# The neighbour sum with every 64th step fetched row by row from SyncE's queue

## The reference

```python
h = jnp.maximum(_layernorm(x, axis=-1), 0.0)
msgs = h[src]
neigh = jax.ops.segment_sum(msgs, dst, num_segments=h.shape[0])
h = (1.0 + eps[0]) * h + neigh
h = jax.nn.relu(h @ W1 + b1)
x = x + (h @ W2 + b2)
```

## Time and profile before

| | us |
|---|---|
| median of 3 runs (4853.4 to 4856.95) | 4854.46 |
| the profiled execution | 4847.91 |
| its span, first to last instruction | 4845.8 |
| GpSimd busy | 3416.4 (71% of the span) |
| DVE busy | 2778.0 (57%) |
| ACT busy | 2159.0 (45%) |
| PE busy | 476.5 (10%) |

### The profile page before, as it was taken

The page is one execution under the profiler, slowest core; times in us unless marked ns, Lnnn a source line. Parts: engine busy times, 40 slices in busy tenths (PEclk is TensorE's granted clock), DMA queues, the critical chain, the costliest instruction groups (busy, mean ns, idle before and its releaser), DMA issues.

```text
span 4845.8 us, 21987 instructions
## 1 busy us (share of the span) xinstructions
PE 476.5 (10%) x2321; PEld 339.9 (7%) x2321; DVE 2778.0 (57%) x4395; ACT 2159.0 (45%) x2238; POOL 3416.4 (71%) x3611
## 2 busy tenths in 40 slices
PE   4620000000000000000189000000000000000005
PEld 2410000000000000000067000000000000000003
DVE  7836888988998988888778222222222222222224
ACT  4414445544455555544367344444444444444431
POOL 4676777777777777777554677777777777777766
PEclk9655555555555555555599555555555555555558
DMA  9995666666666666666455233333333333333324
GB/s 360 382 372 171 211 210 217 212 212 213 213 213 213 214 215 213 214 213 213 139 118 124 94 104 103 103 105 104 103 102 102 102 102 107 103 102 103 104 98 136
DMA packets 235399, 816.50 MB, mean 168 GB/s; under 512 B 67021, under 2 KB 93677, under 8 KB 185162
## 3 DMA queue, kind: packets, MB, share of 16 engines
q1 hardware_dynamic: 77464, 457.58, 24.7%
q0 software_dynamic: 143152, 344.65, 24.3%
q10 hardware_dynamic: 14722, 13.70, 0.9%
HBM read 455.06 MB, written 354.21 MB: 167 GB/s over the span
## 4 chain that ended last, share of the span: by engine, by line
POOL 59%; issue 26%; DMA 8%; PE 5%; DVE 2%; ACT 1%; POOLq 0%; SPq 0%; ACTq 0%; DVEq 0%
POOL arena L632 58%; DMA q_edges<-arena 6%; PE ps L1285 2%; PE ps L1274 2%; DMA arena<-states,node_idx 1%; POOL q_edges L636 0%; PE ps L1306 0%; ACT arena L1119 0%; POOLq L120 0%; PE ps L1265 0%; PE ps L1298 0%; SPq L529 0%; DVE arena L1914 0%; DMA arena<-h_tab,idx 0%; DVE arena L1701 0%
## 5 line engine op out<-in xcount | busy, mean ns | idle before, releaser
L632 POOL DMA_INDIRECT arena<-h_tab,idx x1568 | 1482.0, 945 | 520.5 <-issue 500.2
L632 POOL DMA_INDIRECT arena<-kv_tab,idx x1568 | 1485.1, 947 | 514.5 <-issue 503.5
L1874 DVE SCALAR_TENSOR_TENSOR ps<-arena,keep,ps 128x128 f32<-128x128 f32 x98 | 42.9, 438 | 1500.8 <-ACT ps L1162 1500.8
L1162 ACT COPY ps<-arena 128x2048 f32<-128x2048 f32 x98 | 351.6, 3587 | 948.1 <-DMA arena<-h_tab,idx 948.1
L1066 ACT COPY arena<-arena 128x1024 f32<-128x1024 f32 x196 | 375.6, 1916 | 552.3 <-DVE arena L1701 552.3
L1586 DVE TENSOR_TENSOR_SCAN ps<-arena,ps 128x256 f32<-128x256 f32 (+2 forms) x584 | 501.4, 859 | 0.0
L1169 ACT COPY arena<-arena 128x1024 f32<-128x1024 f32 x196 | 379.1, 1934 | 212.9 <-DVE arena L1882 212.9
L1882 DVE TENSOR_TENSOR_SCAN arena<-arena,ps 128x1024 f32<-128x1024 f32 x196 | 437.5, 2273 | 10.4 <-DVE ps L1874 0.5
L1701 DVE TENSOR_TENSOR_SCAN arena<-arena,ps 128x1024 f32<-128x1024 f32 x196 | 442.9, 2260 | 0.1
L1033 ACT COPY ps<-arena 128x1024 f32<-128x1024 f32 x196 | 363.5, 1887 | 6.1
L1637 DVE TENSOR_TENSOR arena<-arena,ps 128x1024 f32<-128x1024 f32 x196 | 230.4, 1217 | 178.2 <-DMA arena<-kv_tab,idx 178.2
(11 more groups left out here) (240 smaller groups left out, 2380.2 us busy)
## 6 DMA issues: line engine op xcount, KB each, us to landing
states<-arena SPq DMA_DIRECT2D x98, 1152.0 KB, 5.4
q_edges<-arena SPq DMA_DIRECT2D x98, 1024.0 KB, 5.9
arena<-q_edges SPq DMA_DIRECT2D x98, 1024.0 KB, 7.8
states<-arena SPq DMA_DIRECT2D x98, 1024.0 KB, 4.0
arena<-kv_tab,idx POOLq DMA_INDIRECT x1568, 2.8
arena<-h_tab,idx POOLq DMA_INDIRECT x1568, 2.5
kv_tab<-arena ACTq DMA_DIRECT2D x14, 896.0 KB, 11.2
arena<-kv_tab SPq DMA_DIRECT2D x14, 448.0 KB, 5.4
```

Of the source, the lines that this page charges most:

```text
L632: pool.indirect_dma_start(to, None, tab, bass.IndirectOffsetOnAxis(ap=at, axis=0)).then_inc(done, 16)
L1162: nc.scalar.copy(rows_now, rows[k].rearrange("p b f -> p f b")).then_inc(rows_turned, 1)
```

## The change

In each of 24 batches (5, 9, 13, ..., 97: the second of every four, except batch 1) the last of the 16 steps is not gathered by GpSimd. Its 128 rows come through SP, each with a DMA of its own from `h2_tab` to one partition of a small buffer `direct`.

- SP writes the 24 x 128 row numbers once, at the start of stage B, to a table `direct_tab` in memory (L558 of the changed kernel).
- In stage D SP reads 16 of them at a time to registers (`direct_rows`) and issues 16 DMAs of one row. 32 rows stand between two stores. The rows of batch 4q + 5 are fetched while batches 4q to 4q + 2 are stored.
- ACT waits for `direct_in` in those batches, and turns the step and the other 15 with two copies.
- GpSimd's loop now goes over four batches, behind four that are written out.
- Some semaphores of stage C and E are shared (`node_rows_in`, `node_tiles_in`), with counts that go on.

```diff
+QUADS = BATCHES // 4
+DIRECT_AT = 4 * B + 2 * B - 1
+AT_ONCE = 16
+PARTS = P // AT_ONCE
...
+        direct_tab = dram("direct_tab", [QUADS, P], I32)
...
+        direct = cD.two(HID)
+        direct_listed, direct_in = sem("direct_listed"), sem2("direct_in")
...
             sp.dma_start(qb[0], q_rows[:, 0:B, :]).then_inc(q_in[0], 16)
+            sp.dma_start(direct_tab.rearrange("t p -> p t"), src_all[:, DIRECT_AT:STEPS:4 * B], allow_slow_non_contiguous=True)\
+                .then_inc(direct_listed, 16)
...
+            def store_d(n, k):
+                sp.wait_ge(sums_set, n + 1)
+                settle(sp)
+                sp.dma_start(by_step(states1)[:, bass.ds(n * B, B), :], sums_b[k]).then_inc(sums_out[k], 16)
+
+            def direct_rows(q, t, part):
+
+                p0 = part * AT_ONCE
+                src_rows = nc.values_load_multi_w_load_instructions(
+                    direct_tab[bass.ds(q, 1), p0:p0 + AT_ONCE], engines=[mybir.EngineType.SP], min_val=0, max_val=N - 1,
+                    skip_runtime_bounds_check_because="edges name nodes")[1]
+                for r, row in enumerate(src_rows):
+                    sp.dma_start(direct[t][p0 + r:p0 + r + 1, :], h2_tab[bass.ds(row, 1), :]).then_inc(direct_in[t], 16)
+
+            def quads_d(i, first):
+                for t in range(2):
+                    q = i * 2 + t
+                    if not first:
+                        sp.wait_ge(rows_turned, q * 4 - 2)
+                    for r in range(4):
+                        if not (first and t == 0 and r == 0):
+                            store_d(q * 4 + r - 1, (r + 1) % 2)
+                        for part in range(r * PARTS // 4, (r + 1) * PARTS // 4):
+                            direct_rows(q, t, part)
+            sp.wait_ge(direct_listed, 16)
+            for k in range(2):
+                sp.wait_ge(h2_stored[k], 16 * PAIRS)
+            repeat(sp, QUADS // 2, quads_d)
+            for n in range(4 * QUADS - 1, BATCHES):
+                store_d(n, n % 2)
...
-            repeat(pool, BPAIRS, batch_d)
+            for r in range(4):
+                batch_d(r, r % 2, B, r < 2)
+            with pool.Fori(1, QUADS) as i:
+                for r in range(4):
+                    batch_d(i * 4 + r, r % 2, B - (r == 1))
+            for r in range(2):
+                batch_d(4 * QUADS + r, r % 2, B - (r == 1))
...
+                act.wait_ge(rows_in[k], landed)
+                act.wait_ge(sum_s, n * 2 + 1)
+                if direct_t is None:
                     nc.scalar.copy(rows_now, rows[k].rearrange("p b f -> p f b")).then_inc(rows_turned, 1)
+                else:
+                    act.wait_ge(direct_in[direct_t], direct_landed)
+                    nc.scalar.copy(rows_now[:, :, B - 1], direct[direct_t])
+                    nc.scalar.copy(rows_now[:, :, 0:B - 1], rows[k][:, 0:B - 1, :].rearrange("p b f -> p f b"))\
+                        .then_inc(rows_turned, 1)
```

More of the change, by code:

```diff
@@ L57 @@
 EREST = E - EFULL * STEPS
+QUADS = BATCHES // 4
+DIRECT_AT = 4 * B + 2 * B - 1
+AT_ONCE = 16
+PARTS = P // AT_ONCE
+assert BATCHES == 4 * QUADS + 2 and QUADS % 2 == 0
 BPAIRS = BATCHES // 2
@@ L921, in _, with batch_d @@
                 pool.wait_ge(h2_stored[k], 16 * PAIRS)
[L923 to L931, removed]
-            repeat(pool, BPAIRS, batch_d)
+            def batch_d(n, k, steps, peeled=False):
+                pool.wait_ge(idx1_set, n + 1)
+                if not peeled:
+                    pool.wait_ge(rows_turned, n - 1)
+                settle(pool)
+                for b in range(steps):
+                    gather(rows[k][:, b, :], h2_tab, idx[k][:, b:b + 1], rows_in[k])
+            for r in range(4):
[5 more added lines that the diff above has]
+                batch_d(4 * QUADS + r, r % 2, B - (r == 1))
             for k in range(2):
@@ L1155, in _ @@
             keep1_features(0, 0)
[L1157 to L1161, removed]
-                    nc.scalar.copy(rows_now, rows[k].rearrange("p b f -> p f b")).then_inc(rows_turned, 1)
[L1163 to L1171, removed]
@@ L1172, in _, with batch_d @@
-            repeat(act, BPAIRS, batch_d)
+            DIRECT_WAIT = 16 * P
+            def batch_d(n, k, landed, direct_t=None, direct_landed=None, stored=None):
+                act.wait_ge(rows_in[k], landed)
+                act.wait_ge(sum_s, n * 2 + 1)
+                if direct_t is None:
+                    nc.scalar.copy(rows_now, rows[k].rearrange("p b f -> p f b")).then_inc(rows_turned, 1)
+                else:
[3 more added lines that the diff above has]
+                        .then_inc(rows_turned, 1)
+                nc.scalar.copy(idx[k][:], src_all[:, bass.ds((n + 2) * B, B)]).then_inc(idx1_set, 1)
+                keep1_features(n + 1, 1 - k)
+                if stored is not None:
+                    act.wait_ge(sums_out[k], stored)
+                for half in range(2):
+                    act.wait_ge(sum_s, n * 2 + half + 2)
+                    done = nc.scalar.copy(sums_b[k][:, :, half * HF:(half + 1) * HF].rearrange("p b f -> p f b"),
+                                          run_sums[:, half * HF * B:(half + 1) * HF * B].rearrange("p (f b) -> p f b", b=B))
+                done.then_inc(sums_set, 1)
@@ new lines, in quad_d @@
+            def quad_d(i, rows_from, filled, batches=4):
+                for r in range(batches):
+                    n, k = i * 4 + r, r % 2
+                    landed = i * (2 * BW - 16 * k) + (r // 2 + 1) * BW
+                    stored = i * 32 + r // 2 * 16
+                    if r == 1:
+                        batch_d(n, k, landed, rows_from, filled, stored)
+                    else:
+                        batch_d(n, k, landed, None, None, stored)
+            for n in range(4):
+                batch_d(n, n % 2, (n // 2 + 1) * BW, None, None, n // 2 * 16 if n > 1 else None)
@@ L1173, in _ @@
+            with act.Fori(0, QUADS // 2 - 1) as m:
+                for t in range(2):
+                    quad_d(m * 2 + 1 + t, t, m * DIRECT_WAIT + DIRECT_WAIT)
+            quad_d(QUADS - 1, 0, QUADS // 2 * DIRECT_WAIT)
+            quad_d(QUADS, 1, QUADS // 2 * DIRECT_WAIT, 2)
             act.wait_ge(carry1_ps, 1)
```

19 lines of the change are left out of this document (9 added, 10 removed).

## The result

The changed kernel takes 4938.68 us (median of four runs, 4934.74 to 4942.66) where the kernel before takes 4853.93 beside it: a ratio of 1.0174, 95% interval 1.0161 to 1.0186. It is 85 us slower; 341 were forecast. The profiled execution took 4942.66 us, its span is 4941.0.

What follows compares the result with a forecast made beforehand. Stage D was taken as bound by GpSimd's gather queue, then by SP after the change: S = 64.0 + 29.6 + 2.4 + 0.8 = 96.8 us, 24 S - 1982 = +341, 4854.5 + 341 = 5196 us; range 4818 to 5417.

Steps and rivals of the forecast that it cites:

- the prediction's points 2 and 3: Signs in stage D's profile: SP's queue without waits for ACT (2); ACT's copies of sums waiting for a store's landing (3).
- the size of S, 96.8: SP's time for four batches in stage D: 64.0 rows + 29.6 reads + 2.4 stores + 0.8 waits and loop, against GpSimd's 79.7.
- A row at 0.50 us: SP in stage D: one row DMA with register work, 0.45 to 0.76 us; 128 of them take 64.0 us.
- A part at 3.7 us: SP in stage D: 0.8 pointer read + 2.7 list of 16 words + 0.2 arithmetic; eight parts take 29.6 us.
- 24 S - 1982: Change of the whole time in us when SP sets stage D's pace; +341 us with S = 96.8.
- nothing for the table: Stage B: writing 24 x 128 row numbers is covered by some 11 us of slack; 0 us taken, up to 10.
- GpSimd's gain: Stage D: 24 fewer gathers at 1.265 us each take 30.4 us off, if nothing else becomes late.
- the copy on ACT is hidden: Stage D: an added copy of 0.27 us in 24 batches, covered by ACT's 9.5 us idle before each turn.
- `direct_in` is no wait of its own: Rival in stage D that ACT waits for late rows though SP has time; given no chance of its own.
- The rival "SP keeps up": Stage D: S at most 81.3 us, so the full gain of 30.4 and a time of 4824 us; chance 0.19.
- Its own lower neighbour: Argument against SP keeping up: rows at 0.50 and reads of 18.1 us give S 85.3, losing 65 us.
- The sum of 3.8 us for a part: SP's part by the skill page's rule: 18 x 0.2 + 0.2 = 3.8 us, giving S of 97.6.

Runs made afterwards that it cites:

- seven_parts: The changed kernel without the last of eight lists and its 16 row DMAs, so 16 rows are not fetched: 4800.86 us, ratio 0.9913 to the kernel before.
- lists_on_chip: The changed kernel with row-number lists copied by one DMA to the core's own memory and read there, without address reads: 4798.77 us, ratio 0.9909 to the kernel before.
- at_once_8_2: The changed kernel reading 8 row numbers at once instead of 16: 5225.28 us beside 4847.35 of the kernel before, ratio 1.0781.
- table_alone: The changed kernel without SP's rows; GpSimd gathers all 16 steps, the table is still written in stage B: 4853.1 us beside 4843.8, ratio 1.0019.
- at_once_32_2: The changed kernel reading 32 row numbers at once instead of 16: 4810.24 us, ratio 0.9927; the same kernel earlier on a slow chip: 6348 us, 1.185.
- both: The changed kernel with lists in the core's own memory and the table written in stage C, on a slow chip: 6381.6 us, ratio 1.188.

## Why the prediction was right or wrong

*Right: what bounds the stage, and the sign.* SP's time for four batches, S, is above GpSimd's, SP hardly waits, stores come late, ACT waits for them to land and GpSimd for ACT, as the prediction's points 2 and 3 have it. `seven_parts` and `lists_on_chip` show it, and the second leaves the rows and ACT's extra copy as they are, so neither of those is the cause.

*Wrong: the size of S, 96.8 where 86.1 came.* This is the step that failed. Two terms were too large and one too small:

- A row at 0.50 us took 0.41. The DMA instruction alone took 0.228, below all four neighbours (0.252 to 0.566) from which 0.31 was the median; there the 11.5 us of the 128 x 0.09 come from.
- A part at 3.7 us took 3.4: the list 2.03 for 2.7, the pointer 1.11 for 0.8. That is another 2.4 us.
- What is left for stores and the loop, 3.2 us in the prediction, is 86.1 - 52.5 - 27.2 = 6.4, on the other side: -3.2.

11.5 + 2.4 - 3.2 = 10.7. With S = 86.1 the prediction's own 24 S - 1982 gives +84; the profiles differ by 95. That 84 is also the difference of the medians, 85, is luck: the formula holds nothing for the table, and stage D itself grew by 78.2 (SP's last row came 4.6 us sooner than 24 S says, and the turn 1.3 us behind it and not 2.8). The slope of 24 us for each us of S turned an error of 11% into one of 257 us. `at_once_8_2`, with S at 99.1, came out at +378: where S is near what I took it for, the forecast holds to about 5%.

*Wrong: nothing for the table.* I judged the slack by the load of batch 1's queries. The transfer that the words delayed was another, GpSimd's gather of `q_first`, which ACT waited for already (28.7 us before, 38.8 now). The cost, 9 us by `table_alone`, is near the upper end of 10 that I had kept; the first profile has 14.9 ahead of stage D.

*Too small: GpSimd's gain.* 24 x 1.265 = 30.4 held the gaps of the earlier trace rows for a share of every gather. They are stops in every seventh batch, and most of their length went with the change: 24 x 1.25 = 30 and 24 more, 54 in all. In the changed kernel that gain can't be seen, since SP sets the end; it moves the point at which SP stops mattering to GpSimd's 63 x 1.25 = 78.7 us.

*Right: the copy on ACT is hidden* (0.27 us each, as forecast), and `direct_in` is no wait of its own. ACT does wait 250 us for SP's rows, 18 times, but because SP is late with everything: in `lists_on_chip`, where SP has time, it never waits for them.

*The rival "SP keeps up"* was nearer than its 0.19 says. It is true of `lists_on_chip` and `at_once_32_2`. Its own lower neighbour, a row at 0.50 with 18.1 us of reads, S = 85.3 and a loss of 65, is almost what came: 26.4 us of reads, but rows at 0.41.

*The rule on loads.* The Trainium skill, page "Runtime: NRT & Kernel Launch", section "Instruction fetch mechanics", gives about 200 ns for each register. The traces don't agree: 2 words took 1.11 us (0.4 by the rule), 8 took 1.11 (1.6), 16 took 2.03 (3.2), 32 took 4.04 (6.4), and 16 words in the core's own memory 1.32. The four reads from the table fit about 1 us for each eight words begun; no other size was run. The sum of 3.8 us for a part was still near, since the pointer cost more and the list less.

## What to carry to other kernels

Before work is put into the gap of another queue, count everything that the queue then issues and compare the two totals, not the gap with one instruction; where the two are close, give the time as a slope and measure the small instruction first, as 0.09 us stood here 3072 times. Where addresses for register-driven DMAs are read from a table in memory, try the core's own memory: here a few lines turned 1.7% slower into 0.9% faster, and longer lists did nearly as well. Small scattered writes delayed a gather issued behind them on another queue here, so look for the transfer that someone waits for already, and not only at the one next in the program.

## What the runs showed of the hardware

- A read of registers by SP from a table in memory cost the same 1.1 us for 2 and for 8 words, then 2.0 for 16 and 4.0 for 32; 16 words from the core's own memory cost 1.3.
- A DMA of one 512-byte row with its address in a register cost SP 0.41 us from one to the next, 0.23 of them for the DMA instruction, over 3072 rows.
- 3072 words of 4 bytes, written by one DMA, landed 19.9 us after their issue.
- The gathers' queue stops 2.0 to 2.5 us at every 112th gather when all batches have 16, 13 times in each of the stages B and D. With 63 in four batches stage D keeps four to eight stops, most of them of 0.6 to 0.9 us, all in every seventh batch or a multiple of it.
- Two of the five chips of the experiments ran the kernel before 10 to 11% slower, and every kernel with SP's rows 19 to 23% slower than that. The spread of the same SP instruction in `at_once_32` on such a chip, by source line, shows how:

```profile
L616 SPq FUSED_REGOPS  x3072: 1/37/1416, 2997.9 to 6143.1; - x192
L616 SPq DMA_DIRECT2D arena<-h_tab x3072: 1/221/1412, 2998.0 to 6143.2; - x192
```

The medians are those of `at_once_32_2` on the other chip, but in stretches most instructions, register arithmetic too, start 0.7 us or a multiple of it behind the last. The cause stays open: no run here took it apart. The remedies that work on the other chips don't remove it: `both` and `at_once_32` still lost 19% there.
